# Multiplying zeros on TensorE ahead of and between the first bias rows of a feed-forward, attention, feed-forward kernel

## The reference

```python
x = x + 0.5 * ffn(layernorm(x))     # first feed-forward
x = x + attention(layernorm(x))     # 16 heads, 4 key/value heads, causal, rotary
x = x + 0.5 * ffn(layernorm(x))     # second feed-forward, same weights

def ffn(x):                         # 8 experts of 256 x 256, top 2 of 8 by a router
    w = softmax of the two largest of (x @ router_w + router_b), 0 for the other six
    h = silu(x @ expert_w[e] + expert_b[e])        # for each of the 8 experts
    out = (sum over e of w[e] * h[e]) @ proj_w + proj_b
    return norm_w * (x + out) / rms(x + out)
```

## Time and profile before

| | us |
|---|---|
| median of 3 runs | 808.57 |
| lowest, highest | 806.37, 809.85 |
| the profiled execution: time | 807.34 |
| the profiled execution: span | 805.5 |

### The profile page before, as it was taken

The page is one execution under the profiler, slowest core; times in us unless marked ns, Lnnn a source line. Parts: engine busy times, 40 slices in busy tenths (PEclk is TensorE's granted clock), DMA queues, the critical chain, the costliest instruction groups (busy, mean ns, idle before and its releaser), DMA issues.

```text
span 805.5 us, 15700 instructions
## 1 busy us (share of the span) xinstructions
PE 774.1 (96%) x4520; PEld 675.2 (84%) x4520; DVE 628.2 (78%) x1875; ACT 536.4 (67%) x1318; POOL 526.7 (65%) x416
## 2 busy tenths in 40 slices
PE   7899999878999999999999999999999999999996
PEld 3688888667999989999899999998998988788885
DVE  6888996696777777777777777777777887988876
ACT  3555655867677776877778767777687686545543
POOL 4645648975878778777787787777777963412312
PEclk9999999898999999999999999999999999999998
DMA  8145231210131221313311313122121200000001
GB/s 300 70 159 197 95 117 40 53 40 14 40 92 35 69 52 37 93 26 92 91 26 39 91 39 91 45 63 48 42 88 27 53 14 2 1 0 28 13 15 52
DMA packets 30631, 50.12 MB, mean 62 GB/s; under 512 B 3970, under 2 KB 12802, under 8 KB 30594
## 3 DMA queue, kind: packets, MB, share of 16 engines
q1 hardware_dynamic: 30596, 49.71, 21.9%
HBM read 18.76 MB, written 9.96 MB: 36 GB/s over the span
## 4 chain that ended last, share of the span: by engine, by line
POOL 50%; PE 25%; issue 15%; DVE 6%; ACT 2%; POOLq 1%; DMA 1%; ACTq 0%; SPq 0%; DVEq 0%
POOL gc L1314 12%; POOL at_rot L1310 12%; POOL at_rot L1319 11%; POOL at_ql L1302 10%; PE sc L992 3%; PE sc L994 3%; PE sc L993 3%; POOL at_keys L1302 3%; PE pj L992 1%; PE pj L994 1%; PE pj L993 1%; DVE f_acc L514 1%; ACT at_keys L1677 1%; DVE z L427 1%; PE o L992 1%
## 5 line engine op out<-in xcount | busy, mean ns | idle before, releaser
L1720 ACT ACTIVATE at_pr<-at_pr,at_low 128x512 f32<-128x512 f32 (+7 forms) x256 | 135.0, 529 | 49.8 <-DVE at_low L1474 49.5
L1474 DVE CUSTOM_DVE_ANT_0 at_pr<-sc,at_mask 128x512 f32<-128x512 f32 (+2 forms) x192 | 93.2, 521 | 58.7 <-PE sc L1956 58.5
L1302 POOL TENSOR_TENSOR at_ql<-at_rot,at_qh 128x512 fp32r<-128x512 f32 x64 | 83.0, 1297 | 81.8 <-ACT at_qh L1677 81.7
L1730 ACT ACTIVATE at_pr<-at_pr,at_inv 128x512 f32<-128x512 f32 (+7 forms) x256 | 115.9, 524 | 10.9 <-DVE at_inv L1481 10.8
L1487 DVE CAST at_pth<-pt 128x512 fp32r<-128x512 f32 (+1 forms) x188 | 104.6, 596 | 10.8 <-PE pt L1969 10.6
L1319 POOL TENSOR_TENSOR at_rot<-at_rot,gc 128x512 f32<-128x512 f32 x80 | 103.4, 1294 | 10.9
L1496 DVE TENSOR_TENSOR at_ptl<-pt,at_pth 128x512 fp32r<-128x512 f32 x192 | 105.4, 590 | 0.1
L1310 POOL TENSOR_TENSOR at_rot<-ga,cos 128x512 f32<-128x512 f32 x80 | 103.5, 1294 | 2.3 <-POOL at_ql L1302 2.1
L1314 POOL TENSOR_TENSOR gc<-gc,sin 128x512 f32<-128x512 f32 x80 | 103.5, 1295 | 1.2 <-DMA gc<-ga 1.2
L1969 PE MATMUL pt<-ident,at_pr 128*128 128x128 f32 x640 | 88.2, 277 | 4.8 <-issue 2.9
L1969 PEld LDWEIGHTS pt<-ident,at_pr 128*128 128x128 f32 x640 | 76.7, 143 | 12.2 <-issue 3.3
(11 more groups left out here) (280 smaller groups left out, 2227.3 us busy)
## 6 DMA issues: line engine op xcount, KB each, us to landing
gc<-ga SPq DMA_DIRECT2D x160, 128.0 KB, 2.3
ga<-in_attn_w SPq DMA_DIRECT2D x8, 384.0 KB, 4.9
at_wo<-attn_split SPq DMA_DIRECT2D x6, 512.0 KB, 4.1
attn_split<-gb SPq DMA_DIRECT2D x6, 384.0 KB, 2.4
attn_split<-gc SPq DMA_DIRECT2D x6, 384.0 KB, 3.4
gb<-attn_split SPq DMA_DIRECT2D x6, 384.0 KB, 3.6
x<-in_x SPq DMA_DIRECT2D x4, 512.0 KB, 9.2
e_raw<-in_expert_w SPq DMA_DIRECT2D x8, 256.0 KB, 6.1
```

Source lines behind the costliest of these rows:

```text
L1302: pool.tensor_tensor(to, rotated(r), lead.bitcast(F32), ALU.subtract).then_inc(ql_done, 1)
L1474: dve.tensor_tensor_reduce(out=out, in0=sc[bank][:, col:col + w], in1=masked, scale=1.0, scalar=3e38, op0=ALU.add, op1=ALU.min, accum_out= ...
L1720: act.activation(a, a, ACT.Exp, bias=low[kind][:, k:k + 1], scale=-1.0, accum_out=tot[kind][:, k:k + 1]).then_inc(ex_done, 1)
L1730: act.activation(a, a, ACT.Copy, scale=inv[kind][:, k:k + 1]).then_inc(nm_done, 1)
```

## The change

VectorE clears 256 columns of `acc` before everything else. TensorE waits for that, and then issues plain float32 matmuls of those zeros, 128 rows by 128 columns stationary and 256 columns moving, into the bank that `row_of(3)` later overwrites: two before `row_of(0)`, one between `row_of(0)` and `row_of(1)`, three behind `row_of(1)`, in front of batch 0's transposes. Nobody reads what they make.

```diff
             if first:
+                dve.memset(acc[:, 0, :], 0.0).then_inc(setup, 1)
                 dve.memset(r_hl[:].bitcast(F32), 0.0).then_inc(setup, 1)
                 dve.memset(r_h0[:].bitcast(F32), 0.0).then_inc(setup, 1)
...
-                dve.wait_ge(setup, 2)
+                dve.wait_ge(setup, 3)
...
+            def keep_clock(count):
+
+                o = ex_ps[3][:, 0:D]
+                for _ in range(count):
+                    pe.matmul(o, acc[:, 0, 0:P], acc[:, 0, :], start=True, stop=True)
+
...
             if first:
+                pe.wait_ge(setup, 1)
+                keep_clock(2)
                 pe.wait_ge(e_row_in, 16)
                 row_of(0)
+                keep_clock(1)
                 row_of(1)
+                keep_clock(3)
                 pe.wait_ge(ident_in, 16)
                 transpose_first_z()
                 row_of(2)
```

## The result

The changed kernel takes 809.38 us (median of 20 runs, 808.9 to 811.2), the kernel before 806.37 us (20 runs, 805.86 to 809.85): 3.0 us more by the medians, ratio 1.0031, interval 1.0023 to 1.0040. I had forecast 0.4 us less. The three runs of before that I knew had a median of 808.57, 2.2 us above what twenty gave, so my forecast of a time was also built on a base too high; what counts is the difference.

The account below looks back on a forecast made before the run. TensorE bounds it, its 1.2 GHz stretch until about 21.9 us on the path. `zl` 1.65 later at 14.1, plus 9.5, starts GpSimd at 23.6 against 24.10; taken as -0.4, 808.57 becomes about 808.1 us, range 805.2 to 811.3.

Parts of the forecast that it names:

- The clearing costs nothing, TensorE starts at 1.82: Program start: VectorE's clear is covered by idle time until `x` arrives at 4.8; first zeros start at 1.82.
- Six zeros at 0.86 and two rows at 1.75, first transpose 1.95 late: TensorE ahead of batch 0's transposes, slow clock: 1.82 + 5.16 + 3.5 = 10.5 us instead of 8.56.
- Zeros count, two-row matmuls do not, the rise comes near 12: TensorE's clock: three zeros behind `row_of(1)` bring the rise near 12 us, during the transposes; chance 0.50.
- the rule on transposes: Trainium skill's statement that transposes don't count as busy for the clock; by it part of executions fall to 'zeros raise nothing'.
- The rise gives back almost the whole delay: From `zl` to GpSimd's bias addition: `zl` ends 1.65 later at 14.1, plus 9.5 gives 23.6 instead of 24.10.
- 2.1 us are obtainable behind the transposes: End of `zl` to GpSimd's bias addition: VectorE bounds it at 9.5, start 22.0 against 24.10, 2.1 us at most.
- What is late at 24.10 is late at the end: GpSimd's bias addition: what is moved there moves the end too, as later blocks hang on it in one chain.
- zeros raise nothing: Slower rival, TensorE's clock: transposes 1.95 late and the rise later by the same, 810.5 us; chance 0.30.

Follow-up runs that it names:

- clear_only: Changed kernel with VectorE's clearing and the waits kept but no zero matmul issued; 806.65 us, ratio 1.0006 to the kernel before.
- two_row_zeros: Changed kernel with each zero matmul over 2 rows of the cleared operand instead of 128, same places; 811.17 us, ratio 1.0057.
- long_zeros: Changed kernel with fourteen zero matmuls ahead of `row_of(0)` and none elsewhere; 809.13 us in one run, beside 806.16 for the kernel before.
- long_two_row: Changed kernel without zero matmuls or TensorE's wait for `setup`, `row_of(0)`'s two-row matmul issued six times more in front; 817.79 us, one run.
- long_transposes: Changed kernel without zero matmuls, 48 transposes of the zeros in front of `row_of(0)`; 811.89 us in one run, beside 806.16 before.
- again: The changed kernel once more, nothing edited, for a second profile and paired time; 809.13 us, ratio 1.0032 to the kernel before.
- fill_wait: Changed kernel with `row_of(2)` moved ahead of the transposes, and only two zero matmuls, behind the transposes while `zl` is made; 806.38 us, ratio 0.9993.
- third_look: The changed kernel, nothing edited, profiled a third time; that execution took 812.19 us.
- fill_wait_root: Same as fill_wait, plus GpSimd's batch-1 root moved ahead of its shift of pair 3; 806.19 us, ratio 0.9991 to the kernel before.
- before_root: Kernel before with only GpSimd's order changed, batch-1 root ahead of its shift of pair 3; 806.69 us, ratio 0.9999.
- fit_gap: Changed kernel with no zeros ahead of `row_of(0)` or between the rows, two zero matmuls behind them; 807.67 us, ratio 1.0007.

## Why the prediction was wrong

Forecast was 0.4 us less, measured are 3.0 us more. That the measured 809.4 still lies near the forecast time of 808.1 is luck: the base was 2.2 us too high and the change 3.4 us too low.

- *The clearing costs nothing, TensorE starts at 1.82*: right (clear_only; 1.74).
- *Six zeros at 0.86 and two rows at 1.75, first transpose 1.95 late*: too small. It is 3.06 late, 1.05 of it at the changes between two-row and full matmuls, which two_row_zeros takes away. The sum took 1.75 for a row, below both spacings that it had read, 1.87 and 2.00. The 2.00 was that of a row between full matmuls, and the changed kernel's rows take just that.
- *Zeros count, two-row matmuls do not, the rise comes near 12*: the mechanism held (long_zeros, long_two_row), the rise came at 14.1, 13.4 and 11.9 in three of four profiles of this order, in one not at all. I had given the rule on transposes some weight; long_transposes shows the contrary.
- *The rise gives back almost the whole delay*: **this is the step that failed**, on both of its sides. In front, `zl` was to end 1.65 us later; it ends 3.04 later, 15.51 instead of 14.1, as the transposes start 1.1 later than reckoned and still run slow. Behind, the 11.63 us from `zl` to the bias addition were to shrink by 2.1, to 9.5; they shrink by 1.35, to 10.28. Together that makes 25.79 where 23.6 was forecast.
- What holds the stretch behind `zl` at 10.28 in the changed kernel's profile is GpSimd's shift of pair 3. Part of such a block stood in the sum as if it were VectorE's own work, in L454 of before, which takes 0.17 us in the changed kernel:

```profile
18.61 1.22 DVE L454 TENSOR_TENSOR gap<-top 128x4 f32<-128x4 f32 x1
```

- In the changed kernel L415 pays 2.2 us of it instead of L454's 1.05. That the clock fell again, at 17.5, 16.8 and 15.3 in the three profiles, was not forecast either, but costs little: the logits and the tanh come in time in the changed kernel, the tanh 0.18 us late in again, and fill_wait, which keeps the clock, is no shorter behind `zl`. What makes it fall no run isolates. Without the early rise (third_look) the stretch takes 11.54 us, so what the rise gave back is 1.0 to 1.3 us.
- *2.1 us are obtainable behind the transposes*: that was read from one execution whose clock rose late (21.9). In a usual one (clear_only, 19.6) it is 1.2 by the same sum, and fill_wait_root got 0.9 of it. This is the third part of the miss: the profile that I reckoned from began the bias addition 1.2 us later than a usual execution of before, by the time of the median.
- *What is late at 24.10 is late at the end*: right (the table's last column).
- The sum for a usual execution, by what was measured: bias addition at 22.9 before; 3.2 late at the transposes (11.62 against 8.3 to 8.4 in clear_only, before_root and fit_gap); 0.2 to 0.5 given back against before's own rise at 19.6 (clear_only takes 10.74 behind `zl`, the changed kernel 10.28 and 10.54); 25.6 to 25.9, and with 783.5 that is 809.1 to 809.4, as measured. The rival 'zeros raise nothing' was nearer in size (+1.95) and wrong in its reason.

## What to carry to other kernels

Filling TensorE pays only in time in which it waits anyway; the same zeros cost 3 us ahead of the work on the path, and two of them beside a wait cost nothing that is clear of the noise (fit_gap). Ask of a raised clock not only when it comes but which engine takes over the path: here it was VectorE, and the earlier rows also brought GpSimd's shift forward into VectorE's work. Where four numbers per partition take 1.22 us, as in L454, look at what the other engines run beside it before the time goes into a sum as work. Read the base from more than one execution where the clock's rise lies on the path: one profile here was off by as much as the change could bring.

## What was not expected of the hardware

- Float32 matmuls over two rows, 14 us of them in long_two_row (3.0 to 17.0), did not raise the clock, though TensorE was busy throughout; transposes alone did, 3.5 us in, zeros 4.0, ones 6.0 us in.
- A change between two-row and full float32 matmuls costs about 0.15 us on each side of it: a row takes 1.70 us between two-row matmuls, 1.84 with a full one behind it (fill_wait) and 2.00 between full ones.
- A VectorE instruction on four numbers per partition took 2.36 us beside a GpSimd addition of 128 x 1024, and moved the wait to the next one (1.87, 1.95 us) when GpSimd's order was changed.
- The same kernel's executions differ in when the clock rises though nothing in their order differs: three profiles of the changed kernel have it at 14.1, 13.4 and 24.8. What decides it in an execution, and why all of two_row_zeros' times are in the upper group, stays open.
